# Row sums of the attention's first exponential taken by ScalarE instead of VectorE, and a second finD buffer

## Chip, cores and metric
The program runs on all 8 cores of one Trainium2 chip, one batch element of 4096 tokens on each core. The time is the device time in microseconds (us) of the slowest core. The profile and the trace are of one execution, on the core that took longest in it.

## The reference, cut to what matters
Per batch element x is 4096 x 1024. Two blocks are added to it in turn: a global attention with 16 heads and a two-layer local-attention network with feed-forward parts. What matters for the change:

```python
att_num = jnp.exp(jnp.einsum('bhqd,bhkd->bhqk', q_rope, k_rope) * scale)
att_den = jnp.sum(jnp.exp(jnp.einsum('bhqd,bhkd->bhqk', q, k) * scale), axis=-1, keepdims=True)
att = att_num / att_den
y = jnp.einsum('bhqk,bhkd->bhqd', att, v)
...
for l in range(2):
    x = x + o @ wo                     # o: local attention of layer l
    h = layernorm(shift_token(x)) @ w1 + b1
    a, g = jnp.split(h, 2, axis=-1)
    x = x + (a * gelu(g)) @ w2 + b2
```

The numerator uses rotated queries and keys, the denominator plain ones, so the denominator needs a score pass of its own, from which only row sums are kept.

## The kernel before, in words
The program is written by hand, engine by engine: each `@blk.<engine>` function appends its instructions to that engine's queue, so the order on an engine is the order of these functions in the file. Engines meet only in counters: `cT` counts TensorE, `cSL` and `cS` what is named below, `cVc` VectorE; `g_set` names a count and `g_wait` waits for it. `VI` issues a VectorE instruction that counts in `cVc`, and `VW` lets VectorE wait for all that it has counted so far.

`emit_attention` loops over 8 head pairs (`hp`). For each head of a pair (`hh`) it makes the denominator: 32 blocks of 128 queries (`qt`) times 4 stretches of 1024 keys (`ks`), so 128 tiles of 128 x 1024 scores; below, this is "the first pass", and there are 16 of it.
- TensorE (L696) writes a tile with two matmuls of 512 columns into a pair of PSUM banks. Three pairs are used in turn (`next_slot`, `pair=g[0] % 3`); before it writes into one, it waits until `cSL` says that the tile that lay there is done with.
- ScalarE (L713) takes the exponential in place, in PSUM. It waits for `cT` at every second tile only, and then for two tiles at once. It counts in `cS`.
- VectorE (L726) waits for `cS`, sums the 1024 columns of the tile into one column of `denp`, and counts in `cSL`, which frees the pair of banks.
- Behind the 128 tiles VectorE adds the four partial sums of a block (L733 to L738) and takes the reciprocal (L740), TensorE transposes it (L748), VectorE copies it out (L756), and GpSimd stores it to HBM (L763).

Then, for the pair, the "second pass": for 8 blocks of 512 queries, 32 tiles of keys, TensorE makes the rotated scores of both heads (L798, L800), ScalarE takes the exponential into `attb` (L835), and TensorE multiplies it by the values (L811, L814). The sums of the first pass enter through a row that SyncE loads (L779), which L843 and L844 spread over the partitions.

In `emit_ffn_layer`, once per layer, behind the local attention, a loop over 8 slices (`sl`) of 512 tokens makes the output projection and the feed-forward part. SyncE loads the slice's running x into the eight `finD` tiles (L1716) and the attention output into `oTs` (L1718). TensorE projects (L1736), VectorE adds the result into `finD` (L1750), casts it to `xbD` and `sqD` (L1763 to L1770), and, when the row statistics are there (`emit_row_finish`), copies it to `fm13` (L1801). From `fm13` VectorE makes the normalised `hb16` (L1831 to L1835). TensorE multiplies by w1 (L1875, L1878), whose tiles GpSimd loads (L1856, L1858), ScalarE and VectorE make the gated product (L1893, L1902), and TensorE multiplies by w2 (L1920). VectorE adds b2 into `at` (L1931) and `at` into `fm13` (L1933). GpSimd spills `fm13` to `scr_fA` (L1992). In layer 1 VectorE, TensorE and ScalarE make statistics of the result as well, and SyncE stores their rows (L1975) before it comes to the load of the next slice.

Of the kernel before, what the change touches and what calls it, by code (L numbers as in the profile page):

```python
# [10 lines left out]
AF = mybir.ActivationFunctionType  # L11
AX = mybir.AxisListType
# [5 lines left out]
TSL = 512  # L18
# [219 lines left out]
def VI(p, ins):  # L238
    p.cVc.inc(ins, 1)
    return ins  # L240


def VW(p, v):
    v.wait_ge(p.cVc.h, p.cVc.n)
# [11 lines left out]
def g_set(p, key, ctr):  # L256
    p.gates[key] = (ctr, ctr.n)


def g_wait(p, eng, key):  # L260
    ctr, v = p.gates[key]
    eng.wait_ge(ctr.h, v)
# [353 lines left out]
def emit_attention(p):  # L616
    blk = p.blk
    cT, cG, cA, cB = p.cT, p.cG, p.cA, p.cB
    cSL, cRX = p.cSL, p.cRX
# [7 lines left out]
    denp = [p.sbS("S", f"denpS{i}", [128, 128]) for i in range(2)]  # L627
# [30 lines left out]
    for hp in range(8):  # L658
# [18 lines left out]
        slot0 = {}  # L677
        for hh in range(2):
            Q = hq[(hp % 2) * 2 + hh]
            K = hk[(hp % 2) * 2 + hh]  # L680

            @blk.tensor
            def _(t, hp=hp, hh=hh, Q=Q, K=K):
                if hh == 0:
                    g_wait(p, t, ("S_ld", hp))
                    if hp > 0:
                        g_wait(p, t, ("S_ysc", (hp - 1, 7)))
                else:
                    g_wait(p, t, ("S_dnev", (hp, 0)))
                for qt in range(32):  # L690
                    for ks in range(4):
                        bk, _, _ = next_slot(t, pair=g[0] % 3)
                        if qt == 0 and ks == 0:
                            slot0[hh] = g[0]
                        for j in range(2):
                            ins = t.matmul(  # L696
                                bk[:, j * 512:(j + 1) * 512],
                                Q[64:128, qt * 128:(qt + 1) * 128],
                                K[64:128, ks * 1024 + j * 512: ks * 1024 + (j + 1) * 512],
                                start=True, stop=True)  # L700
                        cT.inc(ins, 1)
            g_set(p, ("S_pmm", (hp, hh)), cT)

            @blk.scalar
            def _(s, hp=hp, hh=hh):
                base_t = p.gates[("S_pmm", (hp, hh))][1] - 128
                g0 = slot0[hh]
                for i in range(128):
                    if i % 2 == 0:
                        s.wait_ge(cT.h, base_t + min(i + 2, 128))  # L710
                    gg = g0 + i
                    bk = p.bank(p.slot_pair[gg] * 2, 2)
                    p.cS.inc(s.activation(bk, bk, AF.Exp, scale=0.125), 1)  # L713
            g_set(p, ("S_pexpS", (hp, hh)), p.cS)

            @blk.vector
            def _(v, hp=hp, hh=hh):
                base_s = p.gates[("S_pexpS", (hp, hh))][1] - 128
                g0 = slot0[hh]
                if hh == 0 and hp >= 2:  # L720
                    g_wait(p, v, ("S_invd", (hp - 2, 1)))
                for i in range(128):
                    v.wait_ge(p.cS.h, base_s + i + 1)
                    gg = g0 + i
                    bk = p.bank(p.slot_pair[gg] * 2, 2)
                    cSL.inc(v.reduce_sum(denp[hh][:, i:i + 1], bk, axis=AX.X), 1)  # L726
            g_set(p, ("S_pexp", (hp, hh)), cSL)

            @blk.vector
            def _(v, hp=hp, hh=hh):  # L730
                g_wait(p, v, ("S_pexp", (hp, hh)))
                VW(p, v)
                VI(p, v.tensor_tensor(den[hh][:, :], denp[hh][:, 0:128:4],  # L733
                                      denp[hh][:, 1:128:4], op=OP.add))
                VI(p, v.tensor_tensor(invd[hh][:, :], denp[hh][:, 2:128:4],
                                      denp[hh][:, 3:128:4], op=OP.add))
                VW(p, v)
                VI(p, v.tensor_tensor(den[hh][:, :], den[hh][:, :], invd[hh][:, :], op=OP.add))  # L738
                VW(p, v)
                VI(p, v.reciprocal(invd[hh][:, :], den[hh][:, :]))  # L740
            g_set(p, ("S_invd", (hp, hh)), p.cVc)

            @blk.tensor
            def _(t, hp=hp, hh=hh):
                g_wait(p, t, ("S_invd", (hp, hh)))
                bk, _, _ = next_slot(t)
                p.dnT_slot[(hp, hh)] = g[0]
                cT.inc(t.transpose(bk[0:32, 0:128], invd[hh][:, :], p.ident_f[:, :]), 1)  # L748
            g_set(p, ("S_dnT", (hp, hh)), cT)

            @blk.vector
            def _(v, hp=hp, hh=hh):
                g_wait(p, v, ("S_dnT", (hp, hh)))
                gg = p.dnT_slot[(hp, hh)]
                bk = p.bank(p.slot_pair[gg] * 2, 2)
                cSL.inc(v.tensor_copy(dnstg[hh][:, :], bk[0:32, 0:128]), 1)  # L756
            g_set(p, ("S_dnev", (hp, hh)), cSL)

            @blk.gpsimd
            def _(gp, hp=hp, hh=hh):  # L760
                g_wait(p, gp, ("S_dnev", (hp, hh)))
                cbs = [cB, p.cD[4], p.cD[5], p.cD[0]][(hp % 2) * 2 + hh]
                cbs.inc(gp.dma_start(out=p.scr_dnb[2 * hp + hh, :, :], in_=dnstg[hh][:, :]), 16)  # L763
            g_set(p, ("S_bounceout", (hp, hh)),
                  [cB, p.cD[4], p.cD[5], p.cD[0]][(hp % 2) * 2 + hh])
# [376 lines left out]
def emit_ffn_layer(p, l):  # L1142
    blk = p.blk
    cT, cA, cG, cB = p.cT, p.cA, p.cG, p.cB
    L = f"L{l}_"
# [486 lines left out]
    if l == 1:  # L1632
# [4 lines left out]
    hb16 = [p.sbS(L + "D4", L + f"hb16{c}", [128, TSL], BF16) for c in range(NCH)]  # L1637
    agb = [p.sbS(L + "D4", L + f"agb{i}", [128, TSL], BF16) for i in range(22)]
    gt2 = [p.sbS(L + "D4", L + f"gt{i}", [128, TSL], BF16) for i in range(2)]
    at2 = [p.sbS(L + "D4", L + f"at{i}", [128, TSL]) for i in range(2)]  # L1640
    fm13 = [p.sbS(L + "D4", L + f"fm13{c}", [128, 513]) for c in range(NCH)]
    w1sb = [p.sbS(L + "D4", L + f"w1sb{i}", [128, 8 * 128], BF16) for i in range(4)]
    w2res = [p.sbS(L + "D4", L + f"w2res{i}", [128, 22 * 128], BF16) for i in range(NCH)]
# [6 lines left out]
    wo_sb = [p.sbS(L + "D3", L + f"wo{i}", [128, C], BF16) for i in range(4)]  # L1650
    oTs2 = [p.sbS(L + "D3", L + f"oTs{i}", [128, 4 * TSL], BF16) for i in range(1)]
    finD2 = [[p.sbS(L + "D3", L + f"finD{j}_{c}", [128, TSL]) for c in range(NCH)]
             for j in range(1)]
    carry = [p.sbS(L + "D3", L + f"carry{c}", [128, 1]) for c in range(NCH)]
    carryF = [p.sbS(L + "D3", L + f"carryF{c}", [128, 1]) for c in range(NCH)]
    xbD = [p.sbS(L + "D3", L + f"xbD{c}", [128, TSL], BF16) for c in range(NCH)]
# [42 lines left out]

    for sl in range(NSL):  # L1700
        ssl = slice(sl * TSL, (sl + 1) * TSL)
        finD = finD2[0]
        fmD = finD
        oTs = oTs2[0]

        @blk.sync
        def _(s, sl=sl, ssl=ssl, finD=finD, oTs=oTs):
            g_wait(p, s, L + "F2_done")
            g_wait(p, s, (L, "oTspill"))
            if sl >= 1:  # L1710
                g_wait(p, s, (L + "F3_mmdone", sl - 1))
                g_wait(p, s, (L + "F3_xbsq", sl - 1))
                g_wait(p, s, (L + "F3_fm13", sl - 1))
            cs = [p.cA, p.cE[2]][sl % 2]
            for c in range(NCH):
                cs.inc(s.dma_start(out=finD[c][:, :], in_=p.scr_fA[c, :, ssl]), 16)  # L1716
            for i in range(4):
                cs.inc(s.dma_start(out=oTs[0 * 0][:, i * TSL:(i + 1) * TSL]  # L1718
                                   if False else oTs[:, i * TSL:(i + 1) * TSL],
                                   in_=p.scr_v[i, :, ssl]), 16)  # L1720
# [186 lines left out]
        for oc in range(NCH):  # L1907
            @blk.tensor
            def _(t, sl=sl, oc=oc):
                g_wait(p, t, (L + "F4_ag", (sl, 21)))  # L1910
                if sl == 0 and oc == 0:
                    g_wait(p, t, (L, "w2resld"))
                k = sl * 8 + oc
                if k >= 2:
                    g_wait(p, t, (L + "F4_w2ev", k - 2))
                bk = p.bank(4 + oc % 2)
                buf = w2res[oc]
                for i in range(22):
                    rr = min(128, FHID - i * 128)
                    ins = t.matmul(bk, buf[0:rr, i * 128: (i + 1) * 128],  # L1920
                                   agb[i][0:rr, :], start=(i == 0), stop=(i == 21))
                cT.inc(ins, 1)
            g_set(p, (L + "F4_w2", (sl, oc)), cT)

            @blk.vector
            def _(v, sl=sl, oc=oc):
                g_wait(p, v, (L + "F4_w2", (sl, oc)))
                bk = p.bank(4 + oc % 2)
                at = at2[oc % 2]
                VW(p, v)  # L1930
                VI(p, v.tensor_scalar(at[:, :], bk, b2sb[:, oc:oc + 1], None, op0=OP.add))  # L1931
                VW(p, v)
                VI(p, v.tensor_tensor(fm13[oc][:, 1:513], at[:, :],  # L1933
                                      fm13[oc][:, 1:513], op=OP.add))
            g_set(p, ((L + "F4_w2ev", sl * 8 + oc)) if False else (L + "F4_w2ev", sl * 8 + oc), p.cVc)
# [227 lines left out]
```

## Time and profile before

| what | us |
|---|---|
| timed runs (2): lowest, median, highest | 20103.3, 20134.2, 20165.2 |
| profiled execution | 20223.9 |
| its span on the slowest core | 20222.3 |
| spans of the eight cores | 20106.1 to 20222.3 |
| TensorE busy in the span | 12731.4 (63%) |
| VectorE busy | 7652.6 (38%) |
| ScalarE busy | 5936.7 (29%) |
| attention (1868 to 9260 us of the span) | 7392 |

The profiled execution has 1.6 us around its span. In rows, PE is TensorE (PEld its weight loads), DVE is VectorE, ACT is ScalarE, POOL is GpSimd, SPq is what SyncE queues; `psF` is all of PSUM. "Busy" is the time in which an instruction of the engine was running. PEclk is TensorE's granted clock as a share of 2.4 GHz. In brackets or behind the last bar stands how long the engine was idle before a row, and what ended that idle time.

### The profile page before, as it was taken

The numbers are of one execution on the slowest core, as the hardware profiler recorded it, in microseconds if no ns is written. First come the engines' busy times: TensorE is split into PE (matmuls) and PEld (weight loads), VectorE is DVE, ScalarE is ACT, GpSimd is POOL, SyncE is SP. The second block draws the span as 40 slices with busy tenths as digits, with TensorE's granted clock in tenths as the row PEclk, the third lists the DMA queues.
The fourth block names the chain that finished last, engine by engine and source line by source line (L and its number), as shares of the span: only waits on it lengthen the run. The fifth ranks groups of instructions, "written<-read, shape, count | busy, mean of one in ns | idle before, by whom it ended". The sixth has DMA issues, their size and how long they took to land.

```text
span 20222.3 us, 120771 instructions; the slowest of 8 cores (20106.1 to 20222.3 us)
## 1 busy us (share of the span) xinstructions
PE 12731.4 (63%) x32101; PEld 3109.3 (15%) x32448; DVE 7652.6 (38%) x12808; ACT 5936.7 (29%) x6424; POOL 1319.6 (7%) x2073
## 2 busy tenths in 40 slices
PE   1355677686858687775333677766753577766663
PEld 0111111110101011111111111122221111122221
DVE  1576433425161523323545533122235533122224
ACT  0001555555555555552001111222211111221110
POOL 1131000000000000000000000022210000021110
PEclk9566555555555555555555555588765555577775
DMA  7211000000000000001110000032210000032223
GB/s 106 83 46 40 0 11 0 11 1 11 11 0 11 0 11 0 11 0 50 67 41 20 8 3 3 3 84 78 74 51 19 8 3 3 3 73 63 63 63 104
DMA packets 234777, 625.99 MB, mean 31 GB/s; under 512 B 45476, under 2 KB 61446, under 8 KB 227734
## 3 DMA queue, kind: packets, MB, share of 16 engines
q0 software_dynamic: 125968, 392.23, 8.2%
q1 hardware_dynamic: 98952, 209.25, 3.3%
q10 hardware_dynamic: 9216, 16.78, 0.3%
q8 instruction: 304, 4.98, 0.1%
q14 instruction: 337, 2.76, 0.0%
HBM read 500.24 MB, written 201.88 MB: 35 GB/s over the span
## 4 chain that ended last, share of the span: by engine, by line
PE 46%; DVE 24%; ACT 10%; another core or an unknown queue 6%; issue 6%; DMA 5%; POOL 1%; SPq 1%; DVEq 1%; ACTq 0%; POOLq 0%
DVE denpS L726 6%; PE psF L811 6%; PE psF L798 5%; PE psF L696 5%; ACT psF L713 5%; PE psF L800 4%; PE psF L1920 4%; DMA L_w1sb<-w1bf 3%; PE psF L1875 2%; PE psF L1523 2%; PE psF L1526 2%; PE psF L1530 2%; PE psF L1541 2%; PE psF L1878 2%
## 5 line engine op out<-in xcount | busy, mean ns | idle before, releaser
L696 PE MATMUL psF<-hkS,hqS 64*128 64x512 bf16 x4096 | 2059.1, 605 | 1657.4 <-DVE denpS L726 1490.6
L726 DVE TENSOR_REDUCE denpS<-psF 128x1 f32<-128x1024 f32 x2048 | 2413.4, 1220 | 1343.3 <-ACT psF L713 1342.8
L713 ACT ACTIVATE psF<-psF 128x1024 f32<-128x1024 f32 x2048 | 1971.0, 1006 | 1679.6 <-PE psF L696 1679.4
L835 ACT ACTIVATE attbS<-psF 128x1024 bf16<-128x1024 f32 x2048 | 2090.1, 1024 | 1020.2 <-PE psF L800 1019.5
L811 PE MATMUL psF<-attbS,vpairS 128*64 128x512 bf16 x2048 | 1291.9, 631 | 149.0 <-ACT attbS L835 147.1
L814 PE MATMUL psF<-attbS,vpairS 128*64 128x512 bf16 x2048 | 1302.2, 636 | 0.0
L800 PE MATMUL psF<-hqS,hkS 64*128 64x512 bf16 x2048 | 1291.9, 631 | 0.0
L853 DVE COPY ytmpS<-psF 128x512 f32<-128x512 f32 x64 | 44.3, 692 | 3292.8 <-PE psF L814 3292.8
L798 PE MATMUL psF<-hqS,hkS 64*128 64x512 bf16 x2048 | 1238.3, 605 | 75.8 <-DVE ybuf L861 69.9
L1875 PE MATMUL psF<-L_hb,L_w1sb 128*128 128x512 bf16 (+1 forms) x2759 | 782.4, 432 | 576.6 <-DMA L_w1sb<-w1bf 296.8
L1565 ACT ACTIVATE L_attf<-psF 128x512 bf16<-128x512 f32 x960 | 559.6, 596 | 1107.1 <-PE psF L1530 1038.1
L1576 DVE COPY L_yt<-psF 65x512 f32<-65x512 f32 x128 | 87.9, 686 | 2102.1 <-PE psF L1541 2102.1
L1893 ACT ACT_TABLE_LOAD x352 | 451.6, 1283 | 1468.4 <-PE psF L1878 1468.4
L1902 DVE SCALAR_TENSOR_TENSOR L_agb<-psF,L_b1sb,L_gt 128x512 bf16<-128x512 f32 x352 | 264.1, 750 | 1573.0 <-ACT L_gt L1893 1573.0
L696 PEld LDWEIGHTS psF<-hkS,hqS 64*128 64x128 bf16 x4096 | 277.6, 101 | 3438.3 <-issue 3438.3
L1129 ACT ACT_TABLE_LOAD x48 | 61.6, 1283 | 2513.0 <-DVE srow L1120 2513.0
L1920 PE MATMUL psF<-L_agb,L_w2res 128*128 128x512 bf16 (+1 forms) x2752 | 741.7, 428 | 60.4 <-DVE L_agb L1902 54.6
L1878 PE MATMUL psF<-L_hb,L_w1sb 128*128 128x512 bf16 (+1 forms) x2761 | 757.8, 421 | 4.5 <-issue 0.4
L1565 ACT ACT_TABLE_LOAD x128 | 164.2, 1283 | 1872.3 <-remote 997.0
L1541 PE MATMUL psF<-L_attf,L_vtm 128*65 128x512 bf16 x960 | 601.8, 627 | 166.1 <-ACT L_attf L1565 155.4
L522 PE MATMUL psF<-xhb,w_inT 128*128 128x512 bf16 x1003 | 409.9, 580 | 398.7 <-DVE hbB L548 371.4
L1586 PE MATMUL psF<-L_invloc,ones_rf 1*128 1x512 f32 x256 | 261.2, 1121 | 584.8 <-DVE L_invloc L1579 584.8
(231 smaller groups left out, 14658.9 us busy)
## 6 DMA issues: line engine op xcount, KB each, us to landing
L_w1sb<-w1bf POOLq DMA_DIRECT2D x672, 256.0 KB, 4.0
L_finD<-scr_fA SPq DMA_DIRECT2D x128, 256.0 KB
scr_fA<-L_fm POOLq DMA_DIRECT2D x128, 256.0 KB, 3.7
L_fin<-scr_fA SPq DMA_DIRECT2D x112, 256.5 KB
w1bf<-w POOLq DMA_DIRECT2D x2, 10920.0 KB, 184.9
tm_in<-x SPq DMA_DIRECT2D x32, 512.0 KB
scr_x<-x0T POOLq DMA_DIRECT2D x64, 256.0 KB, 10.4
scr_xh<-x0T POOLq DMA_DIRECT2D x64, 256.0 KB, 3.4
```

The costliest lines, as they stand in the source:

```text
L696: ins = t.matmul(bk[:, j * 512:(j + 1) * 512], Q[64:128, qt * 128:(qt + 1) * 128], K[64:128, ks * 1024 + j * 512: ks * 1024 + (j + 1) * 51 ...
L713: p.cS.inc(s.activation(bk, bk, AF.Exp, scale=0.125), 1)
L726: cSL.inc(v.reduce_sum(denp[hh][:, i:i + 1], bk, axis=AX.X), 1)
L798: t.matmul(bk[:, 0:512], K0[0:64, kt * 128:(kt + 1) * 128], Q0[0:64, qsl], start=True, stop=True)
L800: ins = t.matmul(bk[:, 512:1024], K1[0:64, kt * 128:(kt + 1) * 128], Q1[0:64, qsl], start=True, stop=True)
L811: t.matmul(avb[0:64, :], V[:, k2 * 128: k2 * 128 + 64], att[:, 0:512], start=(k2 == 0), stop=(k2 == 31), tile_position=(0, 0), skip_group_ ...
L814: ins = t.matmul(avb[64:128, :], V[:, k2 * 128 + 64: k2 * 128 + 128], att[:, 512:1024], start=(k2 == 0), stop=(k2 == 31), tile_position=(0 ...
L835: cSL.inc(s.activation(attb[kt % 4][:, :], bk, AF.Exp, scale=0.125), 1)
L1541: ins = t.matmul(avb[0:65, :], vtm[kk[k2]][:, h * 65: h * 65 + 65], attf[f2slot[(h, w, k2)] % 4][:, :], start=(k2 == 0), stop=(k2 == nk - 1))
L1875: t.matmul(ba[0:rr, :], buf_a[:, c * 128: c * 128 + rr], hb16[c][:, :], start=(c == 0), stop=(c == NCH - 1))
L1878: ins = t.matmul(bg[0:rr, :], buf_g[:, c * 128: c * 128 + rr], hb16[c][:, :], start=(c == 0), stop=(c == NCH - 1))
L1920: ins = t.matmul(bk, buf[0:rr, i * 128: (i + 1) * 128], agb[i][0:rr, :], start=(i == 0), stop=(i == 21))
```

## The change
In the first pass the exponential gets an accumulator output: ScalarE writes the tile's row sums itself into the column of `denp`, and the count in `cSL` comes from ScalarE. The VectorE function with the 128 sums is gone; its wait for the reciprocal of two head pairs ago stands on ScalarE now. In the feed-forward loop `finD` has two sets of tiles, used in turn, and the load of a slice waits for the casts and copies of the slice before the last; it still waits for the last projection matmul of the slice before, since `oTs` has one copy. `at` has one buffer in place of two.

```diff
             def _(s, hp=hp, hh=hh):
                 base_t = p.gates[("S_pmm", (hp, hh))][1] - 128
                 g0 = slot0[hh]
+                if hh == 0 and hp >= 2:
+                    g_wait(p, s, ("S_invd", (hp - 2, 1)))
                 for i in range(128):
                     if i % 2 == 0:
                         s.wait_ge(cT.h, base_t + min(i + 2, 128))
                     gg = g0 + i
                     bk = p.bank(p.slot_pair[gg] * 2, 2)
-                    p.cS.inc(s.activation(bk, bk, AF.Exp, scale=0.125), 1)
-            g_set(p, ("S_pexpS", (hp, hh)), p.cS)
-
-            @blk.vector
-            def _(v, hp=hp, hh=hh):
-                base_s = p.gates[("S_pexpS", (hp, hh))][1] - 128
-                g0 = slot0[hh]
-                if hh == 0 and hp >= 2:
-                    g_wait(p, v, ("S_invd", (hp - 2, 1)))
-                for i in range(128):
-                    v.wait_ge(p.cS.h, base_s + i + 1)
-                    gg = g0 + i
-                    bk = p.bank(p.slot_pair[gg] * 2, 2)
-                    cSL.inc(v.reduce_sum(denp[hh][:, i:i + 1], bk, axis=AX.X), 1)
+                    cSL.inc(s.activation(bk, bk, AF.Exp, scale=0.125,
+                                         accum_out=denp[hh][:, i:i + 1]), 1)
             g_set(p, ("S_pexp", (hp, hh)), cSL)
...
-    at2 = [p.sbS(L + "D4", L + f"at{i}", [128, TSL]) for i in range(2)]
+    at2 = [p.sbS(L + "D4", L + f"at{i}", [128, TSL]) for i in range(1)]
...
     finD2 = [[p.sbS(L + "D3", L + f"finD{j}_{c}", [128, TSL]) for c in range(NCH)]
-             for j in range(1)]
+             for j in range(2)]
...
-        finD = finD2[0]
+        finD = finD2[sl % 2]
...
             if sl >= 1:
                 g_wait(p, s, (L + "F3_mmdone", sl - 1))
-                g_wait(p, s, (L + "F3_xbsq", sl - 1))
-                g_wait(p, s, (L + "F3_fm13", sl - 1))
+            if sl >= 2:
+                g_wait(p, s, (L + "F3_xbsq", sl - 2))
+                g_wait(p, s, (L + "F3_fm13", sl - 2))
...
-                at = at2[oc % 2]
+                at = at2[0]
```

VectorE at the start of the first pass of the first head, before (`denpS` are the partial sums, `psF` is PSUM):

```order
L716 UNCONDITIONAL_BRANCH
L726 TENSOR_REDUCE denpS<-psF 128x1 x128
L729 UNCONDITIONAL_BRANCH
L733 TENSOR_TENSOR denS<-denpS 128x32
L735 TENSOR_TENSOR invdS<-denpS 128x32
L738 TENSOR_TENSOR denS<-denS,invdS 128x32
L740 RECIPROCAL invdS<-denS 128x32
```

The first two rows are gone in the changed program; L733 (now L723) is what VectorE does next behind the value spills of the stage before, and it waits for the last count in `cSL`.

ScalarE in the same place, each tile by itself, before:

```order
L713 ACTIVATE psF<-psF 128x1024 [waits cT]
L713 ACTIVATE psF<-psF 128x1024
L713 ACTIVATE psF<-psF 128x1024 [waits cT]
L713 ACTIVATE psF<-psF 128x1024
L713 ACTIVATE psF<-psF 128x1024 [waits cT]
```

and in the changed program:

```order
L715 ACTIVATE psF,denpS0<-psF 128x1024 [waits cT]
L715 ACTIVATE psF,denpS0<-psF 128x1024
L715 ACTIVATE psF,denpS0<-psF 128x1024 [waits cT]
L715 ACTIVATE psF,denpS0<-psF 128x1024
L715 ACTIVATE psF,denpS0<-psF 128x1024 [waits cT]
```

No instruction of ScalarE has moved; each writes a second output, the column of sums, and the wait for TensorE is still at every second one.

SyncE's queue in layer 1, from the load of the first slice to that of the second, in the changed program (`row_rstd` and `row_mr` are the rows of the slice's statistics):

```order
L1709 DMA L_oTs<-scr_v 128x512 x4
L1960 UNCONDITIONAL_BRANCH
L1966 DMA scr_r<-row_rstd 1x512 [waits cVc]
L1966 DMA scr_r<-row_mr 1x512
L1696 UNCONDITIONAL_BRANCH
L1707 DMA L_finD_0<-scr_fA 128x512 [waits cSL,cD0,cT]
```

Before, the same rows stand in the same order (as L1718, L1969, L1975, L1706 and L1716), and the last waits for `cVc` too. Only that wait has gone; the place on the queue is the same.

## Rows read from the trace of the kernel before

**Rows 1.** The page: span; groups with busy us, mean ns of one, idle before
```profile
span 20222.3 us, 120771 instructions; the slowest of 8 cores (20106.1 to 20222.3 us)
...
L696 PE MATMUL psF<-hkS,hqS 64*128 64x512 bf16 x4096 | 2059.1, 605 | 1657.4 <-DVE denpS L726 1490.6
L726 DVE TENSOR_REDUCE denpS<-psF 128x1 f32<-128x1024 f32 x2048 | 2413.4, 1220 | 1343.3 <-ACT psF L713 1342.8
L713 ACT ACTIVATE psF<-psF 128x1024 f32<-128x1024 f32 x2048 | 1971.0, 1006 | 1679.6 <-PE psF L696 1679.4
L835 ACT ACTIVATE attbS<-psF 128x1024 bf16<-128x1024 f32 x2048 | 2090.1, 1024 | 1020.2 <-PE psF L800 1019.5
```

**Rows 2.** Attention: length, busy PE, PEld, DVE, ACT, POOL, then PEclk, DMA, GB/s
```profile
1868.00:9260.00 7392.00, 5451.55 (x12560) 895.38 (x12560) 2564.04 (x2320) 4163.80 (x4176) 8.77 (x18) 0.50 0.02 6
```

**Rows 3.** Timeline of a first pass: start us, length us, row
```profile
1999.42 1.93 ACT L713 ACTIVATE psF<-psF 128x1024 f32<-128x1024 f32 x2 [1.66 <-PE psF L696]
...
2000.53 2.36 DVE L726 TENSOR_REDUCE denpS<-psF 128x1 f32<-128x1024 f32 x2 [1.23 <-ACT psF L713]
...
2001.90 2.14 PE L696 MATMUL psF<-hkS,hqS 64*128 64x512 bf16 x4 [1.45 <-DVE denpS L726]
...
2003.00 1.93 ACT L713 ACTIVATE psF<-psF 128x1024 f32<-128x1024 f32 x2 [1.66 <-PE psF L696]
...
2010.17 1.93 ACT L713 ACTIVATE psF<-psF 128x1024 f32<-128x1024 f32 x2 [1.66 <-PE psF L696]
```

**Rows 4.** Timeline: start of the first pass, and of the second head's
```profile
1870.68 2.71 PE L696 MATMUL psF<-hkS,hqS 64*128 64x512 bf16 x6 [29.21 <-DMA vpairS<-scr_v]
1871.06 0.14 PEld L696 LDWEIGHTS psF<-hkS,hqS 64*128 64x128 bf16 x1 [0.28 <-issue]
1871.49 0.14 PEld L696 LDWEIGHTS psF<-hkS,hqS 64*128 64x128 bf16 x1 [0.28 <-issue]
...
2105.82 2.71 PE L696 MATMUL psF<-hkS,hqS 64*128 64x512 bf16 x6 [0.64 <-DVE dnstgS L756]
```

**Rows 5.** Timeline of a second pass, one of ScalarE's exponentials
```profile
2599.80 1.02 ACT L835 ACTIVATE attbS<-psF 128x1024 bf16<-128x1024 f32 x1 [0.51 <-PE psF L800]
```

**Rows 6.** Table by stretches, as rows 2: w2 matmuls of layer 0; a second pass
```profile
13404.00:13414.00 10.00, 10.00 (x46) 4.21 (x45) 2.89 (x4) 0.00 (x0) 0.00 (x0) 1.00 0.01 2
...
2450.00:2650.00 200.00, 187.06 (x465) 34.28 (x464) 8.24 (x12) 118.89 (x116) 0.00 (x0) 0.50 0.00 1
```

**Rows 7.** ScalarE's other groups, each shape apart
```profile
L1565 ACT ACTIVATE L_attf<-psF 128x512 bf16<-128x512 f32 x960 | 559.6, 596 | 1107.1 <-PE psF L1530 1038.1 <-remote 46.2 <-PE psF L1541 21.4
...
L713 ACT ACT_TABLE_LOAD x16 | 20.5, 1283 | 1100.2 <-PE psF L696 1100.2
...
L1131 ACT ACTIVATE rowA_rstd<-srow 1x512 f32<-1x512 f32 x16 | 10.1, 628 | 1.7 <-ACT srow L1129 0.4
```

**Rows 8.** Layer 0: timeline; GB/s of 13440 to 13500 in 40 slices
```profile
13438.81 1.70 PE L1736 MATMUL psF<-L_oTs,L_wo 128*128 128x512 bf16 x7 [0.38 <-issue]
...
13467.88 3.81 SPq L1716 DMA_DIRECT2D L_finD<-scr_fA  x8
...
13495.01 1.89 PE L1875 MATMUL psF<-L_hb,L_w1sb 128*128 128x512 bf16 x8 [2.52 <-DMA L_w1sb<-w1bf]
...
13633.16 1.90 PE L1736 MATMUL psF<-L_oTs,L_wo 128*128 128x512 bf16 x8
...
GB/s 257 180 109 188 254 76 0 0 0 0 0 0 0 0 0 0 11 0 0 75 178 253 399 409 360 75 0 0 0 0 0 0 0 0 153 183 123 238 8 0
```

**Rows 9.** Layer 1: SyncE's timeline, and who L1736 waits for (us, times)
```profile
18267.58 0.24 SPq L1975 DMA_DIRECT2D scr_r<-row_rstd  x1
...
18268.43 4.58 SPq L1716 DMA_DIRECT2D L_finD<-scr_fA  x8
...
  DMA L_oTs<-scr_v: 127.4, 7
```

**Rows 10.** The line L1931: who it waits for (us, times)
```profile
  PE psF L1920: 582.5, 128
```

## The prediction

> **What bounds the kernel now.** I read the page first for the costliest lines, then the stages, then one stretch of the attention in order of time, then the stages that the second half of the diff touches. The page [rows 1] gives a span of 20222.3 us. Its three top rows of the first score pass form a ring: the sum L726 waits for the exponential L713 (1342.8 us), L713 for the matmul L696 (1679.4), L696 for L726 (1490.6). Nobody in that ring is the bottleneck; they take turns. The table of stages [rows 2] says that the attention is 7392 us of the span, at a granted clock of 0.50, the lower of TensorE's two levels (1.2 GHz).
>
> How the turns go is in [rows 3]. Two exponentials start at 1999.42, the next two at 2003.00, 2006.59 and 2010.17: a period of (2010.17 - 1999.42) / 3 = 3.583 us for two tiles of 1024 columns. Inside a period: ScalarE starts at 1999.42; VectorE starts the first sum at 2000.53 (1.11 later: 1.006 for the exponential [rows 1], 0.10 to hand over); TensorE starts at 2001.90 (1.37 later: 1.22 for the sum, 0.15 to hand over); ScalarE's next pair at 2003.00 (1.10 later). 1.11 + 1.37 + 1.10 = 3.58. The reason is in the code: three pairs of banks, ScalarE waits once for two tiles, and the second of these can only be written when the sum has freed the first pair of banks of the three.
> A pass has 64 such periods: 64 x 3.583 = 229.3 of the 235.14 us between two starts (1870.68 to 2105.82, [rows 4]); there are 16 passes (8 head pairs x 2), so 1024 periods and 3669 us.
>
> The second pass of the attention, L798 to L835, has its own pace: ScalarE works 1.02 us and is idle for 0.51 before it [rows 5], a tile in 1.53, while TensorE is busy 187.06 of 200 us [rows 6]. No line of it changes.
>
> **The change part by part.**
>
> *The sum goes into the exponential.* 2048 sums of 1.22 us (2413.4 us of VectorE) go. The period loses 1.37 - 0.15 = 1.22 us for the sum itself and one hand-over of 0.10; the hand-over of 0.15 stays, since TensorE now waits for ScalarE. What comes in is an unknown: after each exponential ScalarE must write one column of sums to SBUF. No row of before shows that. Call its price r, the time from a tile's start until its banks are free E, and the time from one tile's start to the next S. The new period is the longer of two paths:
> - ring: E + 0.15 + 1.10, one exponential, the hand-over, then TensorE's stretch up to ScalarE's next pair;
> - ScalarE alone: 2 S.
>
> Bounds of r. Below: nothing, when the sums come out with the exponential. Then E = 1.006, and two exponentials in a row take 1.93 for 2.01 of durations [rows 3], so S = 0.925; the ring decides with 2.26 us. It can't be below that, as the exponential itself does not get shorter. Above: the shortest ScalarE operation of the trace, 0.628 us [rows 7], behind a complete exponential with no overlap: E = S = 1.634, and 2 S = 3.27 decides. Between them I take the row that is nearest in kind, the fixed part of an exponential that writes to SBUF: 1.024 us for 1024 columns [rows 1], 0.596 for 512 [rows 7], so 0.428 for 512 columns and 0.168 for none. With r = 0.168 behind a complete exponential E = 1.174; the ring gives 1.174 + 0.15 + 1.10 = 2.42, ScalarE alone at most 2 x 1.174 = 2.35. The ring still decides, narrowly. The saving is 3.583 - 2.42 = 1.162 us a period, x 1024 = **1190 us**.
>
> By the Trainium skill, "ScalarE: Activation LUTs", section "What ACT_TABLE_LOAD costs", an exponential with immediate scale takes 186 ns plus 0.833 ns a column and neighbours overlap by some 93 ns. The row of 1006 ns for 1024 columns lies 33 ns under that and the overlap of 0.08 us is near it; for one column the rule would give r = 0.187, a period of 2.44 and 18,964 us as an estimate, 20 us above mine.
>
> *Ends of a pass.* The last sum of a pass ended the wait of L733; now the last exponential does. That gain is the 64th period's and is counted. Table load, first three tiles, reciprocal, transpose: unchanged, 6 us a pass. The wait for ("S_invd", (hp - 2, 1)) moves from VectorE to ScalarE, once a head pair, for a reciprocal that was done before the whole last head pair began: nothing. Behind it would stand the exponentials, if it ever held.
>
> *Second copy of finD.* The load of a slice no longer waits for this slice's casts and copies, only for its last L1736 matmul. In layer 0 it is issued at 13467.88 and TensorE wants it at 13633.16, where it starts without a wait for a DMA [rows 8]: 165 us of cover, so being 27 us earlier (the slice's last L1736 matmuls end at 13440.5) gives nothing. It then shares the DMA engines with the spill of the slice before and the first w1 tiles. Before, these are through by 13449 and nothing moves for the 19 us behind them (six slices of 1.5 us with traffic, then empty ones, [rows 8]); the load itself, 8 x 256 KB and 4 x 128 KB, takes some 10 us of traffic, which goes into the empty stretch. If it held up a w1 tile once a slice by the 2.52 us that such a wait takes [rows 8], 7 slices would lose 18 us; I take 0, and keep 18 for the range. In layer 1 the load is late: TensorE waits 127.4 us for it at 7 slices [rows 9], and there it would pay. But on SyncE's queue it stands behind L1975, which waits for the end of the slice: issued at 18267.58, the load at 18268.43 [rows 9]. The row of the changed program is in the same place. Gain 0.
>
> *One at buffer instead of two.* L1931 is idle only for the matmul before it (582.5 us, 128 times, [rows 10]), and both writes already wait for everything earlier on VectorE: 0.
>
> **Sum.** The profiled execution took 20223.9 us; less 1190 it is 19034. The two timed runs (20103.3 and 20165.2) have their median at 20134.2, 90 below the profiled one. The same saving gives **18,944 us**, -5.9%. A measurement tells about 2% from no change here, 403 us.
>
> **Rivals.**
>
> 1. *ScalarE becomes the bound, the sum is dear.* r at 0.628: 3.583 - 3.268 = 0.315 x 1024 = 323 us saved, 19,811. For: nothing of ScalarE in the trace is shorter. Against: those rows all have 512 columns, which are most of their time. 5%.
>
> 2. *Slower.* Between exponentials ScalarE has to change state, at the price of the one such row there is, the table load of 1.283 us [rows 7]. S = 1.006 + 1.283 = 2.289, period 4.58, +0.995 x 1024 = +1019, 21,153. Any r above (3.583 - 2.012) / 2 = 0.785 us makes the kernel slower. For: a second kind of instruction stands after each exponential, and ScalarE would have no idle time left. Against: the load is there 16 times for 2048 exponentials, once at the start of a pass. 4%.
>
> 3. *The granted clock rises.* With less waiting TensorE is denser. At a clock of 1.00 46 matmuls take 10.00 us, 0.22 each [rows 6], against 0.43 from one to the next at 0.50 [rows 4]; TensorE's 1.10, with two of them in it, becomes 0.68, the ring 2.00, and 2 S = 2.35 decides: 1.235 x 1024 = 1265, 18,869. If the second pass rose too, its 1.53 would go to ScalarE's 1.02, 0.51 x 2048 = 1044 more, 17,825. Against: in the second pass TensorE is busy 94% at a granted clock of 0.50 [rows 6], denser than the first pass can become (four matmuls of 0.43 us in 2.42). 4% and 2%. The Trainium skill, "TensorE: Matmul & The Clock Gate", Part 1, says that sustained activity releases the gate to 2.4 GHz; by its words the busy second pass should be there already, and this trace does not agree.
>
> 4. *The double buffer does more than I see*, and frees layer 1's 127 us: 18,944 - 127 = 18,817. Against: the place on SyncE's queue. 3%.
>
> **How the numbers follow.** The forecast (r from 0 to twice 0.168 without overlap) has 82%. Its ends: r = 0 gives (3.583 - 2.256) x 1024 = 1359, 18,775; r = 0.336 gives S = 1.342, 2 S = 2.68, 0.899 x 1024 = 921, 19,213. With the +-31 us of the two runs and the 18 us of the second part: 18,740 to 19,300. Rivals 3 (first half) and 4 lie inside. Faster by over 2%: 82 + 4 + 2 + 3 = 91%; within 2%: rival 1, 5%; slower: rival 2, 4%.
>
> **What would show it.** In the changed profile: pairs of exponentials 2.42 us apart; no VectorE row in the first pass but the four of the reciprocal; a short ScalarE row of 0.1 to 0.2 us after each exponential; L696 idle for ScalarE instead of VectorE, and ScalarE still idle some 0.1 us a pair. A period of exactly 2 S with no such idle time says ScalarE bound, and that r is over 0.2. A pass of 235.14 - 64 x 1.162 = 161 us. Granted clock 0.50 up to the end of the attention. The L1736 matmuls wait for the load as before: not at all in layer 0 after its first slice, about 127 us in layer 1. I am wrong if the short row is above 0.34 us or if the second pass's 1.53 us changes.

## The result, and the profile after

The changed kernel takes 18,934.3 us (median of 11 runs, 18,881.5 to 19,000.8); the kernel before takes 20,184.1 us (median of 10 runs, 20,103.3 to 20,304.8). The ratio is 0.9383, with a 95% interval of 0.9359 to 0.9408: 1250 us less, 6.2% faster. The forecast was 18,944 us in a range of 18,740 to 19,300. That it came within 10 us is partly luck, as said below.

The profiled execution took 18,879.5 us, with a span of 18,877.9 on core 5. First the page, with the groups that answer to [rows 1] (busy us, mean ns of one, idle time before and what ended it); L715 is the old L713, L825 the old L835:

```profile
span 18877.9 us, 119066 instructions; the slowest of 8 cores (18781.4 to 18877.9 us)
...
L825 ACT ACTIVATE attbS<-psF 128x1024 bf16<-128x1024 f32 x2048 | 2090.1, 1024 | 1020.0 <-PE psF L790 1019.2
L696 PE MATMUL psF<-hkS,hqS 64*128 64x512 bf16 x4096 | 2058.8, 605 | 424.7 <-ACT psF L715 358.1
L715 ACT ACTIVATE psF<-psF 128x1024 f32<-128x1024 f32 x2048 | 2072.6, 1012 | 226.5 <-PE psF L696 226.3
```

The VectorE group of 2413.4 us is gone, and the three waits of the old ring (1342.8, 1679.4, 1490.6 us) have become two of 226.3 and 358.1. The new instruction is too small for the page; ScalarE's groups, each shape apart, have it:

```profile
L715 ACT ACTIVATION_READ_ACCUMULATOR psF<-psF 128x1 f32 x2048 | 389.3, 190 | 0.0
```

So the unknown price r of the prediction is 0.190 us. How it lies in the period is read from the timeline of a first pass, which answers to [rows 3]:

```profile
1999.17 1.01 ACT L715 ACTIVATE psF<-psF 128x1024 f32<-128x1024 f32 x1 [0.22 <-PE psF L696]
...
2000.09 0.20 ACT L715 ACTIVATION_READ_ACCUMULATOR psF<-psF 128x1 f32 x1
2000.18 1.02 ACT L715 ACTIVATE psF<-psF 128x1024 f32<-128x1024 f32 x1
...
2000.43 2.04 PE L696 MATMUL psF<-hkS,hqS 64*128 64x512 bf16 x4 [0.33 <-ACT psF L715]
...
2001.53 1.01 ACT L715 ACTIVATE psF<-psF 128x1024 f32<-128x1024 f32 x1 [0.22 <-PE psF L696]
...
2006.26 1.01 ACT L715 ACTIVATE psF<-psF 128x1024 f32<-128x1024 f32 x1 [0.22 <-PE psF L696]
```

The short row starts at 2000.09, before the exponential's row ends (1999.17 + 1.01 = 2000.18), and the next exponential starts at 2000.18, before the short row ends at 2000.29. So a tile's banks are free E = 2000.29 - 1999.17 = 1.12 us after its start, and the next tile starts S = 1.01 after it. From 2000.29 TensorE starts after 0.14, ScalarE's next pair 1.10 later: 1.12 + 0.14 + 1.10 = 2.36, and (2006.26 - 1999.17) / 3 = 2.363. Two tiles at a distance of 1.01 would take ScalarE 2.02, and it is idle for 0.22 us before each pair (the forecast was some 0.1). The ring decides, and not narrowly. The last tiles of a pass and the start of the next (compare [rows 4]):

```profile
2024.76 0.19 ACT L715 ACTIVATION_READ_ACCUMULATOR psF<-psF 128x1 f32 x1
2025.12 0.21 DVE L723 TENSOR_TENSOR denS<-denpS 128x32 f32<-128x32 f32 x1 [180.57 <-ACT psF L715]
...
2027.48 2.71 PE L696 MATMUL psF<-hkS,hqS 64*128 64x512 bf16 x6 [0.64 <-DVE dnstgS L746]
```

VectorE sits idle for 180.57 us before L723: nothing of the pass is left on it. The first pass starts at 1870.7 as before, so it is 156.8 us instead of 235.1: 78.3 x 16 = 1253 us.

The attention as a whole is a clean measure, since TensorE runs at one level of its clock there. From the first L696 to the first matmul by w_out (L967, before L977), rows of those lines by themselves (count, min/median/max ns, first and last start). After:

```profile
L696 PE MATMUL psF<-hkS,hqS x4096: 579/627/631, 1870.7 to 7544.6; 64*128 64x512 bf16 x196
...
L967 PE MATMUL psF<-ybuf,w_outT x512: 379/379/634, 8046.9 to 8971.0; 128*128 128x512 bf16 x171
```

and before:

```profile
L977 PE MATMUL psF<-ybuf,w_outT x496: 379/437/634, 9303.1 to 10239.8; 128*128 128x512 bf16 x166
```

That is 8046.9 - 1870.7 = 6176.2 us, against 9303.1 - 1870.7 = 7432.4: 1256 us less. The eight cores have 6172 to 6176 us after and 7429 to 7434 before. The table by stretches has the attention and a piece of a second pass (columns as in [rows 2], which the first row answers; the second answers [rows 6]):

```profile
1868.00:8004.00 6136.00, 5451.17 (x12560) 896.42 (x12560) 150.71 (x272) 4385.42 (x6224) 9.11 (x18) 0.50 0.02 7
...
2250.00:2450.00 200.00, 190.71 (x482) 34.20 (x480) 6.19 (x9) 123.05 (x120) 0.00 (x0) 0.50 0.00 1
```

TensorE's busy time in the attention did not change (5451.55 before), it only waits less, and its granted clock stayed at 0.50 (1.2 GHz). The second pass kept its pace: L825 is busy for 2090.1 us and idle for 1020.0 before its rows, as L835 was (2090.1 and 1020.2).

What lies behind the attention took 10,741 to 10,831 us on the eight cores after and 10,808 to 10,919 before. The next section says why the difference is not put down to the change.

The second half of the change did what the queue order says: nothing. In layer 0 TensorE does not wait for the load after the first slice; in layer 1 the load still stands behind the store of the rows (SyncE's timeline, answers to [rows 9]; the last row is who L1727, the old L1736, waits for in layer 1, us and times):

```profile
16971.05 0.35 SPq L1966 DMA_DIRECT2D scr_r<-row_mr  x1
16971.71 3.65 SPq L1707 DMA_DIRECT2D L_finD<-scr_fA  x8
...
  DMA L_oTs<-scr_v: 120.3, 7
```

It was 127.4 us at 7 slices.

### The profile page after: what moved, and what is told of

Read it like the earlier page. It is cut to its first block, busy times and chain, and to the rows that moved or that the text cites. A ratio compares the mean times of both kernels' runs of the same rounds, so it can differ in the third digit from the quotient of the medians.

```text
span 18877.9 us, 119066 instructions; the slowest of 8 cores (18781.4 to 18877.9 us)
## 1 busy us (share of the span) xinstructions
PE 12699.5 (67%) x32448; PEld 3092.3 (16%) x32448; DVE 5239.6 (28%) x10760; ACT 6158.8 (33%) x8472; POOL 1316.4 (7%) x2073
## 4 chain that ended last, share of the span: by engine, by line
PE 50%; DVE 21%; ACT 11%; issue 8%; DMA 5%; another core or an unknown queue 2%; POOL 1%; SPq 1%; DVEq 1%; ACTq 0%; POOLq 0%
ACT psF L715 6%; PE psF L801 6%; PE psF L788 6%; PE psF L696 6%; PE psF L790 4%; PE psF L1911 4%; DMA L_w1sb<-w1bf 3%; PE psF L1866 2%; PE psF L1520 2%; PE psF L1513 2%; PE psF L1516 2%; DVE L_invloc L1569 2%; PE psF L1531 2%; PE psF L1869 2%
## 5 line engine op out<-in xcount | busy, mean ns | idle before, releaser
L825 ACT ACTIVATE attbS<-psF 128x1024 bf16<-128x1024 f32 x2048 | 2090.1, 1024 | 1020.0 <-PE psF L790 1019.2
L696 PE MATMUL psF<-hkS,hqS 64*128 64x512 bf16 x4096 | 2058.8, 605 | 424.7 <-ACT psF L715 358.1
L715 ACT ACTIVATE psF<-psF 128x1024 f32<-128x1024 f32 x2048 | 2072.6, 1012 | 226.5 <-PE psF L696 226.3
L1866 PE MATMUL psF<-L_hb,L_w1sb 128*128 128x512 bf16 (+1 forms) x2816 | 767.4, 422 | 614.5 <-DMA L_w1sb<-w1bf 331.7
L1869 PE MATMUL psF<-L_hb,L_w1sb 128*128 128x512 bf16 (+1 forms) x2816 | 718.4, 401 | 0.0
L723 DVE TENSOR_TENSOR denS<-denpS 128x32 f32<-128x32 f32 x16 | 3.4, 214 | 2504.1 <-ACT psF L715 2504.1
L696 PEld LDWEIGHTS psF<-hkS,hqS 64*128 64x128 bf16 x4096 | 278.7, 101 | 2204.3 <-issue 2204.3
```

The source lines that it names most:

```text
L696: ins = t.matmul(bk[:, j * 512:(j + 1) * 512], Q[64:128, qt * 128:(qt + 1) * 128], K[64:128, ks * 1024 + j * 512: ks * 1024 + (j + 1) * 51 ...
L715: cSL.inc(s.activation(bk, bk, AF.Exp, scale=0.125, accum_out=denp[hh][:, i:i + 1]), 1)
L825: cSL.inc(s.activation(attb[kt % 4][:, :], bk, AF.Exp, scale=0.125), 1)
L1866: t.matmul(ba[0:rr, :], buf_a[:, c * 128: c * 128 + rr], hb16[c][:, :], start=(c == 0), stop=(c == NCH - 1))
L1869: ins = t.matmul(bg[0:rr, :], buf_g[:, c * 128: c * 128 + rr], hb16[c][:, :], start=(c == 0), stop=(c == NCH - 1))
```

## Experiments

"Attention" below is the span from the first L696 to the first matmul by w_out. It is read from each core; all cores of a run agree within 5 us.

The experiments ran in two series, in which the kernel before had medians of 20,213.5 us (e1 to e4) and 20,235.4 us (e5 to e9), against 20,184.1 in the result. So whole times and ratios to before do not say quite the same when a run is compared with the changed kernel: for e5 and e7 they differ by 50 to 80 us. Where a stage can be read by itself, its span is the better measure.

### The two halves apart

`e1_sum_only` is the changed kernel with finD, its waits and `at` as before (the two lines of `at` go back as well):

```diff
-             for j in range(2)]
+             for j in range(1)]
...
-        finD = finD2[sl % 2]
+        finD = finD2[0]
...
-            if sl >= 2:
-                g_wait(p, s, (L + "F3_xbsq", sl - 2))
-                g_wait(p, s, (L + "F3_fm13", sl - 2))
+                g_wait(p, s, (L + "F3_xbsq", sl - 1))
+                g_wait(p, s, (L + "F3_fm13", sl - 1))
```

> Only the first half of the change (row sums by ScalarE); finD, its waits and the at buffers as before. Theory (ring): all of the gain is the ring of the first pass, 1.22 us less in each of 1024 periods, so this takes the time of the changed kernel, 18,934 us within 20. Rival (the second finD buffer gives the 59 to 97 us by which the stages behind the attention were shorter in the profile after): 18,990 to 19,030.

Measured: 18,948.4 us (18,902.0 to 18,964.9), ratio to before 0.9373 (0.9345 to 0.9400); attention 6172 to 6177 us.

`e2_find_only` is the kernel before with that part of the change alone, the same lines the other way round.

> Only the second half of the change (two finD sets, later waits, one at buffer); the sums stay on VectorE. Theory: nothing, 20,184 us within 20, and TensorE waits as long for the load in layer 1 as before (127 us at 7 slices on one core). Rival (the buffer is worth 59 to 97 us): 20,090 to 20,125.

Measured: 20,189.6 us (20,135.1 to 20,276.0), with 20,213.5 for the kernel before in the same series, ratio 0.9988 (0.9970 to 1.0007); attention 7431 to 7434 us.

The first half alone has the whole gain: its ratio 0.9373 and the change's 0.9383 are within each other's intervals. The second half alone is not distinguishable from nothing; its interval would still allow up to 0.3% (60 us). TensorE's waits for the load did not change either: over both layers 206.1 us at 9 slices in e2, 209.6 at 9 before. That the changed kernel was shorter behind the attention as well is no sign of the second buffer: e1, with one finD, took 10,750 to 10,915 us there on its eight cores, e2, with two, 10,777 to 10,886, before 10,808 to 10,919. On e1's cores the longest of these times had a lower mean granted clock than the shortest (0.594 on the core of 10,915, 0.603 on that of 10,750), though the order is not strict: the lowest, 0.592, is on the core of 10,868.

A closer comparison is the stretch of layer 1 from the first projection matmul of its first slice to that of its last, on cores at about the same granted clock there. On the cores with a mean of 0.826 to 0.835 in it, before took 1671 to 1687 us, e2 1668 to 1685, e1 1664 and 1677, the changed kernel 1664 to 1679. The second buffer is worth no more than some 10 us there.

### What the ring is made of

`e3_wait_each` changes one line of the changed kernel, so that ScalarE starts a tile when that tile is there:

```diff
-                    if i % 2 == 0:
-                        s.wait_ge(cT.h, base_t + min(i + 2, 128))
+                    s.wait_ge(cT.h, base_t + i + 1)
```

> The changed kernel, but ScalarE waits for TensorE at each tile of the first pass, for that tile alone, not at every second for two. Theory (the ring decides, because ScalarE waits for two tiles with three pairs of banks): the ring now covers three tiles (2.36 / 3 = 0.79 us a tile), ScalarE alone is the bound at 1.01 to 1.02 us a tile, so 2.04 for two instead of 2.36: 0.32 x 1024 = 330 us less, 18,604. ScalarE has no idle time left in the pass. Rival (ScalarE already bounds at 2.36 with its sum instruction, or each wait costs as much as it saves): 18,934, no change.

Measured: 18,642.5 us (18,607.4 to 18,668.5), ratio to before 0.9227 (0.9200 to 0.9255); attention 5850 to 5855, 323 us less than the changed kernel's 6174. The timeline of its first pass, and its ScalarE group:

```profile
2000.59 1.00 ACT L714 ACTIVATE psF<-psF 128x1024 f32<-128x1024 f32 x1
...
2001.53 0.18 ACT L714 ACTIVATION_READ_ACCUMULATOR psF<-psF 128x1 f32 x1
2001.62 1.00 ACT L714 ACTIVATE psF<-psF 128x1024 f32<-128x1024 f32 x1
...
2002.65 1.00 ACT L714 ACTIVATE psF<-psF 128x1024 f32<-128x1024 f32 x1
```

```profile
L714 ACT ACTIVATE psF<-psF 128x1024 f32<-128x1024 f32 x2048 | 2054.2, 1003 | 0.2
```

A tile every 1.03 us and 0.2 us of idle time in 2048 tiles: now ScalarE is the bound, and it was not in the changed kernel, whose tiles take 1.18.

`e4_before_wait_each` is the same edit in the kernel before, with the sums on VectorE.

> The kernel before, the sums on VectorE, but ScalarE waits for each tile alone. Theory: the slow pace of before was the ring, not VectorE's 1.22 us sums: the ring of 3.58 us then covers three tiles, 1.19 a tile, and VectorE's sums follow each other at 1.13; 2.39 for two tiles, 1.19 x 1024 = 1222 us less than before, 18,962, nearly the gain of the whole change. Rival (the sums themselves are the bound and moving them is what gains): 20,184, no change, or at best what VectorE's idle time of 1.31 us a period allows.

Measured: 18,958.0 us (18,933.5 to 19,012.5), ratio 0.9389 (0.9360 to 0.9417); attention 6216 to 6220 us. Its timeline and VectorE's group:

```profile
1999.43 2.14 ACT L712 ACTIVATE psF<-psF 128x1024 f32<-128x1024 f32 x2 [0.31 <-PE psF L696]
...
2000.95 3.27 PE L696 MATMUL psF<-hkS,hqS 64*128 64x512 bf16 x6 [0.48 <-DVE denpS L725]
...
2002.06 3.27 ACT L712 ACTIVATE psF<-psF 128x1024 f32<-128x1024 f32 x3 [0.48 <-PE psF L696]
...
2004.54 1.01 PE L696 MATMUL psF<-hkS,hqS 64*128 64x512 bf16 x2 [0.31 <-DVE denpS L725]
...
L725 DVE TENSOR_REDUCE denpS<-psF 128x1 f32<-128x1024 f32 x2048 | 2385.5, 1219 | 157.2 <-ACT psF L712 91.7
```

TensorE starts its runs at 2000.95 and 2004.54, 3.59 us apart, and six matmuls, three tiles, lie between them: the length of the old ring, but for three tiles in place of two, 1.20 us a tile. VectorE still makes all 2048 sums, and its idle time before them fell from 1343.3 us to 157.2. One changed wait takes 1215 us off the attention (7432 to 6217), the change 1258 (7432 to 6174). So the sums on VectorE were not what made the pass slow by themselves: the ring of exponential, sum and matmul was, because it was walked once for two tiles and could be walked once for three. With each tile waited for alone, moving the sums is worth 365 us (6217 in e4, 5852 in e3), not 1258. No run changes the number of pairs of banks.

`e5_no_sums` measures what the sum instruction adds to the ring. It leaves out the row sums: the denominators are a constant.

```diff
-                    cSL.inc(s.activation(bk, bk, AF.Exp, scale=0.125,
-                                         accum_out=denp[hh][:, i:i + 1]), 1)
+                    cSL.inc(s.activation(bk, bk, AF.Exp, scale=0.125), 1)
...
                 g_wait(p, v, ("S_pexp", (hp, hh)))
+                if hp == 0:
+                    VI(p, v.memset(denp[hh][:, :], 1.0e18))
```

> The changed kernel without any row sums: the exponential has no accumulator output, and the partial sums are a constant that VectorE writes once per head, so the softmax's denominators are left out; the wait of ScalarE is at every second tile, as in the change. Theory (ring of exponential + sum + hand-over + two matmuls): the sum instruction adds to the ring only what it ends later than the exponential, 0.11 us (1.12 against 1.006), so the period is 1.006 + 0.14 + 1.10 = 2.25 in place of 2.36 and the time 0.11 x 1024 = 116 us less, 18,820. Rival (the whole 0.19 us of the sum instruction is on the path for each of the 2048 tiles): 389 us less, 18,545.

Measured: 18,832.0 us (18,734.7 to 18,898.1), ratio 0.9294 (0.9261 to 0.9328); attention 6063 to 6067, 109 us less than the changed kernel (the medians say 102). In its timeline:

```profile
2001.09 1.93 ACT L715 ACTIVATE psF<-psF 128x1024 f32<-128x1024 f32 x2 [0.33 <-PE psF L696]
...
2003.35 1.93 ACT L715 ACTIVATE psF<-psF 128x1024 f32<-128x1024 f32 x2 [0.33 <-PE psF L696]
```

The period is 2.26 us, the lower bound of the prediction. The sum instruction, 389 us of busy time, costs 109 us of the end: once a period, the part by which it ends after the exponential.

### The load of layer 1

`e7_load_first` gives the load of a slice the place before the store of the rows. The store's block is now a function, called behind the load of the next slice, and for the last slice where it stood:

```diff
+        if l == 1 and sl >= 1:
+            spill_rows(sl - 1)
...
+            if sl == NSL - 1:
+                spill_rows(sl)
```

> The changed kernel, and in layer 1 SyncE issues the load of a slice before it stores the rows of the slice before (that store moves behind the load). Theory: the place on SyncE's queue, and not the single finD, kept the load late; now it is issued early in the slice before, the 7 waits of 18.2 us go, 18,934 - 127 = 18,807. Rival (the load would collide with the w1 tiles, or what follows has another wait of the same length): 18,934, no change.

Measured: 18,842.2 us (18,815.3 to 18,896.3), ratio to before 0.9312 (0.9291 to 0.9333), against the change's 0.9383. The answer for the tile oTs in layer 1, who L1740 waits for, and the timeline where a slice ends and the next begins:

```profile
  DMA L_oTs<-scr_v: 40.6, 1
  DVE L_finD L1754: 34.9, 10
```

```profile
17169.21 2.47 PE L1964 MATMUL psF<-L_sq,inv_c 128*1 128x512 bf16 x8
17171.62 1.90 PE L1740 MATMUL psF<-L_oTs,L_wo 128*128 128x512 bf16 x8
17178.55 8.38 PE L1740 MATMUL psF<-L_oTs,L_wo 128*128 128x512 bf16 x24 [5.03 <-DVE L_finD L1754]
```

The 7 waits for the DMA are gone (the one of 40.6 us is the layer's first slice), but TensorE runs into VectorE instead, 5.03 us at a slice, 34.9 in all: VectorE's rows of the slice before still stand ahead of its first addition (the last of them, L1127, starts at 17177.01, after 2.98 us of waiting for ScalarE, and the addition, L1754, at 17177.62). The 127 us expected came out as 120.3 - 34.9 = 85 by the waits, and 92 by the medians. The ratios to before would make it 143, with intervals that allow some 60 either way. In the stretch of layer 1 used above, e7 took 1579 to 1616 us on its eight cores and the changed kernel 1664 to 1731; e7's two cores with a mean clock of 0.82 there (1601, 1603) are 61 to 78 us below the changed kernel's six at 0.83 (1664 to 1679), so 85 is nearer than 127.

`e8_load_first_one_find` is the same with one finD set, its earlier waits and two `at` buffers.

> As e7_load_first, but with one finD set, its earlier waits and two at buffers as before (the first half of the change is in). Theory: with one finD the load is free to go once the slice before has copied it to fm13, early in the slice, with over 150 us of cover, so this is as fast as e7, 18,807. Rival (the second finD is needed once the queue lets the load go): 18,934, as without the new place.

Measured: 18,868.0 us (18,826.3 to 18,893.7), ratio 0.9314 (0.9294 to 0.9334), not distinguishable from e7. In layer 1's stretch, on the cores with a mean clock of 0.837 to 0.847 there, e7 took 1579 to 1594 us and e8 1582 to 1592. The second set of finD has no worth that shows even when the queue lets the load go; the wait for the copies to fm13 ends early in a slice. In e8 the load starts 35 us behind the store of the rows (17003.43 and 17038.07), in e7 9 us behind it (16952.34 and 16961.62), and two loads of e8 are 238 us apart.

### The fastest version

`e9_both` has the edits of e3 and of e7.

> The changed kernel with both: ScalarE waits for each tile of the first pass alone (as e3) and layer 1's load stands before the store of the rows (as e7). If the two are independent: 18,642 - 127 = 18,515, the fastest version. Rival (they are not, or e7 gives nothing): 18,642.

Measured: 18,540.2 us (18,515.5 to 18,574.1), ratio to before 0.9155 (0.9138 to 0.9172); attention 5849 to 5853 us. It beats both kernels, and the two edits add up: by the medians it is 102 us below e3, where e7 was 92 below the change, and by the ratios 0.0072 and 0.0071.

## Why the prediction was right

- **What bounds the first pass.** Right as read: a ring of three engines, walked once in two tiles. e4 shows it without touching the sums, and e5 and e3 take the ring apart.
- **The size of the saving.** Predicted 1.162 us a period and 1190 us; measured 1.22 us a period by the timeline, 1249 us, and 1256 on the attention. The term that was mis-sized is E. Its price r was taken as 0.168 and is 0.190, but it was put behind the complete exponential (1.174), and the sum instruction starts some 0.09 us before the exponential's row ends: E is 1.12. The prediction's own rows had such an overlap between two exponentials (0.08 us, S = 0.925 for 1.006), and it was left out of E. The two errors pull in opposite directions, and the second is larger.
- **ScalarE alone.** Predicted at most 2.35 us for two tiles, so that the ring would decide "narrowly". It is 2.06 (e3). The margin was 0.3 us, which is what e3 then collected.
- **The time.** 59 us less was saved in the forecast than in the measurement, and the median of before, taken from two runs at 20,134, is 20,184 over ten. The two differences nearly cancel; the hit of 10 us says less than the 60 us of the saving.
- **The Trainium skill's figures** for a ScalarE instruction ("ScalarE: Activation LUTs", "What ACT_TABLE_LOAD costs") gave 0.187 us for one column; the row has 0.190, though it is of another instruction. The overlap of some 93 ns that the section states for exponentials in a row shows here between the exponential and the sum instruction too, 0.08 to 0.11 us on either side. Had the sum used it for E, these figures would give, as an estimate, 1.006 + 0.187 - 0.093 = 1.10 us and a period of 2.35; 1.12 and 2.36 were measured.
- **The second half.** Right, and for the reason given: layer 1's load stands behind L1975 on SyncE's queue. e7 shows it by moving it. "Nothing" is shown to 0.3% by e2's interval, and to some 10 us in layer 1's stretch. TensorE's 7 waits in layer 1 were forecast at 127 us and are 120.3. The 19 us that the prediction calls empty in layer 0 have one slice of 11 GB/s in them, which changes nothing.
- **Rivals.** A dear sum (0.628 us) and a change of state at each tile (1.283) fell with the row of 0.190 and the 16 table loads, as before. The granted clock stayed at 0.50. Rival 1's price was not the shortest ScalarE operation, as it says: the 0.596 us of [rows 7] is shorter and would have given 19,746 in place of 19,811. Rival 4 was false for the second finD, but about 85 of its 127 us were there for another edit.

## What to carry to other kernels

When three engines wait for each other in turn, add up the ring before moving work: the period is the ring's length divided by the number of tiles that may be in it, and a wait that is taken for two tiles at once can cost as much as an operation. Here one changed wait (e4) gave nearly what moving 2048 sums gave (1215 and 1258 us), and both together (e3) gave 320 us more. A second buffer helps only if the wait it removes is the last one in front of the load; look at what stands ahead on the issuing queue first.

## What the runs showed that I had not expected

The accumulator's result is a ScalarE instruction of its own, 185 to 195 ns each in the changed kernel, that overlaps the exponentials on both sides: it lengthens the distance of two exponentials from 0.925 us to 1.01 to 1.03, about 0.1 us, though its rows show 0.19. And the work behind the attention, with nearly the same instructions in before, the changed kernel and e1 to e5, took from 10,741 to 10,919 us on different cores and runs, with mean granted clocks of whole cores from 0.583 to 0.605, so a change of under 1% in this kernel is better read from a stage at a steady clock than from the whole.
